# Casting each projection result one tile later in VectorE's order

## The chip, the cores and the metric

The kernel runs on all 8 cores of one Trainium2 chip. Each core computes half of the queries of one of four sequences; the cores don't talk to each other. The metric is the device time in microseconds of the slowest core. Beside the kernel's time a profile of one execution is shown.

## The reference, cut

```python
# x (4, 8192, 1024); Wq, Wk (512, 1024), 8 heads of 64; Wv (8192, 1024)
def attn(x):
    Q = (x @ Wq.T).reshape(b, n, 8, 64)
    K = (x @ Wk.T).reshape(b, n, 8, 64)
    V = (x @ Wv.T).reshape(b, n, 8, 1024)
    a = softmax(einsum('bnhr,bmhr->bhnm', Q, K))
    return einsum('bhnm,bmhd->bnd', a, V)
x = x + layernorm(attn(layernorm(x)))
x = x + layernorm(ffn(layernorm(x)))   # two token-mixed inputs, gate, squared relu
```

## The kernel before

The program is one list of instructions per engine, written out in order; engines meet only at semaphores. `V` is VectorE (DVE), `A` ScalarE (ACT), `T` TensorE (PE), `SY` the SP queue and `G` the POOL queue, both of which only issue DMAs. `V.call(..., chain=True)` also waits for V's own previous instruction. `rec` remembers the semaphore value at which a named step is done, and `waitp(rec[...])` waits for it.

Four phases follow each other, with a meeting of all engines between some of them. Phase 0 transposes the weights. Phase 1, the one that the change touches, handles 97 tiles of 128 tokens: 64 tiles of the whole sequence, for K, and 33 of the core's queries, for Q. Phase 2 is attention, phase 3 the feed-forward part.

For tile idx phase 1 does this:
- SP loads the f32 tile (512 KB) into one of 6 buffers `xf`; the load of tile idx waits for the normalization of tile idx-6 (`lncopy`).
- Layernorm in four steps: `ln_s1` (DVE: two bn_stats, one bn_aggr), `ln_s2` (ACT: Ln and Exp for 1/sigma), `ln_s3` (DVE: a 128x1 product, `nmr`), `ln_s4` (ACT: the bf16 tile, into `x_ln` or `qlnb`).
- `p1_tr` (PE): 8 transposes of 128x128 into PSUM banks 2 and 3. They wait for the tile's `lncopy` and for `p1eg` of tile idx-1, that is, for DVE to have copied the previous transposes out.
- `p1_stage`, first half (DVE): two copies of 512 columns from banks 2 and 3 into `xlt[idx % 4]`, each recorded as `p1eg`.
- `p1_mm` (PE): 32 matmuls of 128 columns into bank 4 + idx % 4. They wait for `p1eg` of the tile and for `p1stage` of tile idx-4.
- `p1_stage`, second half (DVE): waits for the matmuls (`p1mm`), and for tile 8g (K) or each even Q tile also for the writes of the group before, then casts the bank into `ktstage` or `qtstage` (`p1stage`).
- After 8 K tiles, or 2 Q tiles, POOL's queue writes the staging buffer to HBM with 4 DMAs and waits until they have landed (`skw`). There is one `ktstage` and one `qtstage`.

The loop in `emit_scalar_vector` is a software pipeline: turn i has `ln_s1` of tile i, `ln_s2` of i-1, `ln_s3` of i-2, `ln_s4` of i-3 and `p1_stage` of i-4. PE's list is `p1_tr(0)`, and then for each idx `p1_tr(idx + 1)`, `p1_mm(idx)`.

All instructions are recorded with the line of one helper, so the profile's rows are told apart by tile names: `pb` is a PSUM bank, `identb` the identity of the transposes, `wkT_p` and `wqT_p` the projection weights.

Of the kernel before, what the change touches and what calls it, by code (L numbers as in the profile page):

```python
# [332 lines left out]
def ln_s1(V, A, M, rec, key, src, par):  # L333
    st6 = M["stats6"][:, par * 12:par * 12 + 12]
    war = rec[("lnae", key[0], key[1] - 4)] if key[1] >= 4 else None
    half = src.shape[-1] // 2
    V.call("bn_stats", st6[:, 0:6], src[:, 0:half], chain=True, inc=None)
    V.waitp(war)
    V.call("bn_stats", st6[:, 6:12], src[:, half:2 * half], chain=True, inc=None)
    V.call("bn_aggr", M["stats2"][:, par * 2:par * 2 + 2], st6, chain=True,  # L340
           inc=None)
    rec[("lnagg", key[0], key[1])] = V.prev


def ln_s2(V, A, M, rec, key, par):
    A.waitp(rec[("lnagg", key[0], key[1])])
    A.call("activation", M["rstd"][:, par:par + 1],
           M["stats2"][:, par * 2 + 1:par * 2 + 2], AF.Ln,
           bias=M["consts"][:, 0:1], chain=True, inc=None)
    A.call("activation", M["rstd"][:, par:par + 1], M["rstd"][:, par:par + 1],  # L350
           AF.Exp, scale=M["consts"][:, 1:2], chain=True, inc=None)
    rec[("lnae", key[0], key[1])] = A.prev


def ln_s3(V, A, M, rec, key, par):
    V.waitp(rec[("lnae", key[0], key[1])])
    if key[1] >= 4:
        V.waitp(rec[("lncp", key[0], key[1] - 4)])
    V.call("tensor_scalar", M["nmr"][:, par:par + 1],
           M["stats2"][:, par * 2:par * 2 + 1], -1.0, M["rstd"][:, par:par + 1],  # L360
           ALU.mult, ALU.mult, chain=True, inc=None)
    rec[("lnnm", key[0], key[1])] = V.prev


def ln_s4(V, A, M, rec, key, src, dst, par):
    A.waitp(rec[("lnnm", key[0], key[1])])
    A.call("activation", dst, src, AF.Identity, bias=M["nmr"][:, par:par + 1],
           scale=M["rstd"][:, par:par + 1], chain=True, inc=None)
    rec[("lncp", key[0], key[1])] = A.prev


def emit_scalar_vector(A, V, M, rec):
# [28 lines left out]
    NP1 = NK + NTILE  # L401

    def p1_src(i):
        return M["xf"][(i + 4) % 6][:]

    def p1_dst(i):
        return (M["x_ln"][:, i * 1024:(i + 1) * 1024] if i < NK
                else M["qlnb"][i % 4][:])

    def p1_stage(idx):  # L410
        for par in range(2):
            V.waitp(rec[("p1tr", idx, 6 + par)])
            V.call("tensor_copy",
                   M["xlt"][idx % 4][:].rearrange("p (j2 two b) -> p j2 two b",
                                                  two=2, b=128)[:, :, par, :],
                   M["banks"][2 + par][:].bitcast(BF16)[:, 0:512].rearrange(
                       "p (c b) -> p c b", b=128),
                   chain=True, inc=None)
            rec[("p1eg", idx, par)] = V.prev
        V.waitp(rec[("p1mm", idx)])  # L420
        pbk = banks[4 + idx % 4]
        if idx < NK:
            V.wait("skw", 16 * (M["NKW0"] + 4 * (idx // 8)))
            g = idx % 8
            dst3 = M["ktstage"][:].rearrange("p (a f) -> p a f", a=4)[:, :, g * 128:(g + 1) * 128]
        else:
            qi = idx - NK
            V.wait("skw", 16 * (M["NKW0"] + 32 + 4 * (qi // 2)))
            dst3 = M["qtstage"][:].rearrange("p (a f) -> p a f", a=4)[:, :, (qi % 2) * 128:(qi % 2) * 128 + 128]
        src3 = pbk[:].rearrange("p (a f) -> p a f", a=4)  # L430
        V.call("tensor_copy", dst3, src3, chain=True, inc=None)
        rec[("p1stage", idx)] = V.prev

    for i in range(NP1 + 4):
        if i < NP1:
            V.wait(f"lxf{(i + 4) % 6}", 16 * (i // 6 + 1))
            ln_s1(V, A, M, rec, ("p1", i), p1_src(i), i % 4)
        if 0 <= i - 1 < NP1:
            ln_s2(V, A, M, rec, ("p1", i - 1), (i - 1) % 4)
        if 0 <= i - 2 < NP1:  # L440
            ln_s3(V, A, M, rec, ("p1", i - 2), (i - 2) % 4)
        if 0 <= i - 3 < NP1:
            j = i - 3
            if j >= NK and j - 4 >= NK:
                A.waitp(rec[("p1tr", j - 4, 7)])
            ln_s4(V, A, M, rec, ("p1", j), p1_src(j), p1_dst(j), j % 4)
            rec[("lncopy", j)] = rec[("lncp", "p1", j)]
        if 0 <= i - 4 < NP1:
            p1_stage(i - 4)

    A.waitp(A.prev)
    A.call("nop", inc="sph")
# [348 lines left out]
def build():  # L801
# [191 lines left out]
    A0 = Eng("a", counts, "safo")  # L993
    V0 = Eng("v", counts, "svo")
    emit_scalar_vector(A0, V0, M, rec)
    emit_dma(Eng("s", counts, "ld"), Eng("g", counts, "skw"), M, rec)
    totals = dict(counts)
# [5 lines left out]
    Ar = Eng("a", counts2, "safo", record=True)  # L1003
    Vr = Eng("v", counts2, "svo", record=True)
    emit_scalar_vector(Ar, Vr, M, rec)
    Sr = Eng("s", counts2, "ld", record=True)
    Gr = Eng("g", counts2, "skw", record=True)
# [70 lines left out]
```

How the kernel before makes its waits and increments, by code:

```python
def replay(eng, sems, ops):  # L92
    for op in ops:
        if op[0] == "w":
            eng.wait_ge(sems[op[1]], op[2])
        else:
            _, meth, args, kwargs, sem, dinc = op
            ins = getattr(eng, meth)(*args, **kwargs)
            if sem is not None:
                ins.then_inc(sems[sem], dinc)
```

## Time and profile before

| | us |
|---|---|
| runs of the kernel | 12242.71 and 12708.11, median 12475.41 |
| profiled execution | 12247.06 |
| its span on the slowest core (shown) | 12245.5 |
| its spans on the 8 cores | 12231.0 to 12245.5 |
| mean granted TensorE clock, all cores | 0.944 |

The span runs from the first to the last instruction of a core. Busy times are of instructions alone, without waits. Matmuls are pipelined, so that a row's mean duration is longer than the distance between two of them. The granted clock is a share of 2.4 GHz: 1.00 is that level, 0.50 is 1.2 GHz. The rows of a timeline merge neighbouring instructions of a kind, and in brackets stands how long the engine was idle before them and what it waited for.

### The profile page before, as it was taken

How to read it: one execution, taken by the hardware profiler on the slowest of the kernel's cores; microseconds unless marked ns; L12 is line 12 of the kernel's file. 1: busy time of each engine (PE TensorE's matmuls, PEld its weight loads, DVE VectorE, ACT ScalarE, POOL GpSimd, SP SyncE). 2: the span in 40 equal slices, each digit the busy share in tenths (PEclk: the TensorE clock that was granted, in tenths of full speed). 3: DMA queues.
4: the chain of work that ended last, by engine and by line, in shares of the span. 5: the costliest groups of instructions: out<-in, count | busy, mean ns of one | idle time of the engine just before them, and what ended most of it. 6: DMA issues, size and time to landing. Idle time of an engine off the chain costs nothing.

```text
span 12245.5 us, 243677 instructions; the slowest of 8 cores (12231.0 to 12245.5 us)
## 1 busy us (share of the span) xinstructions
PE 10725.1 (88%) x89784; PEld 7880.7 (64%) x89784; DVE 5608.9 (46%) x12826; ACT 3302.1 (27%) x9514; POOL 93.9 (1%) x180
## 2 busy tenths in 40 slices
PE   3555999999999999999999999999999999999354
PEld 2444777777676767676767676767676767677222
DVE  4433444444444444444444444444444444445554
ACT  0222222222222222222222222222222222223322
POOL 0001000000000000000000000000000000000000
PEclk9666999999999999999999999999999999999677
DMA  7221111111111111111111111111111111112311
GB/s 237 88 78 60 45 46 47 46 47 47 47 47 47 46 47 46 48 46 48 46 48 46 46 47 43 50 42 52 40 53 41 53 40 53 39 54 79 100 42 49
DMA packets 695446, 681.03 MB, mean 56 GB/s; under 512 B 592448, under 2 KB 608960, under 8 KB 657664
## 3 DMA queue, kind: packets, MB, share of 16 engines
q1 hardware_dynamic: 678592, 595.56, 16.9%
q0 software_dynamic: 15680, 69.87, 1.4%
q8 instruction: 730, 11.96, 0.4%
q14 instruction: 444, 3.64, 0.1%
HBM read 595.44 MB, written 69.86 MB: 54 GB/s over the span
## 4 chain that ended last, share of the span: by engine, by line
PE 85%; DVE 8%; issue 2%; ACT 2%; DMA 2%; DVEq 0%; SPq 0%; ACTq 0%; POOL 0%; POOLq 0%
PE pb L98 85%; DVE stats L98 2%; DVE outsb L98 2%; DVE xlt L98 1%; DVE wstage L98 1%; DMA wvt_s<-wstage 1%; DMA xmb<-xm_s 1%; DVE xrT L98 0%; DVE xkT L98 0%; DVE d L98 0%; DVEq L95 0%; ACT rstd L98 0%; ACT krelu L98 0%; DVE ktstage L98 0%; ACT rgate L98 0%
## 5 line engine op out<-in xcount | busy, mean ns | idle before, releaser
L98 PE MATMUL pb<-pt,x_ln 128*128 128x256 bf16 (+1 forms) x69632 | 8165.2, 271 | 0.0
L98 PEld LDWEIGHTS pb<-pt,x_ln 128*128 128x128 bf16 x69632 | 6331.0, 98 | 1187.4 <-issue 5.4
L98 ACT ACTIVATE pt<-pb 128x256 bf16<-128x256 f32 (+1 forms) x8704 | 2811.8, 374 | 7202.3 <-PE pb L98 5920.2
L98 DVE TENSOR_TENSOR dacc<-dacc,pt 128x256 f32<-128x256 f32 (+1 forms) x8568 | 3576.6, 417 | 1850.6 <-ACT pt L98 1051.8
L98 DVE CAST yt<-pb 128x256 bf16<-128x256 f32 (+1 forms) x1088 | 453.6, 417 | 2633.6 <-PE pb L98 2633.6
L98 PE MATMUL pb<-qtb,ktb 64*128 64x256 bf16 (+1 forms) x8704 | 1221.6, 277 | 178.3 <-ACT pt L98 156.1
L98 PE MATMUL pb<-wvtb,yt 128*128 128x512 bf16 x4224 | 954.3, 379 | 246.9 <-DVE outsb L98 246.9
L98 PEld LDWEIGHTS pb<-qtb,ktb 64*128 64x128 bf16 x8704 | 418.1, 93 | 1072.7 <-issue 1048.0
L98 PEld LDWEIGHTS pb<-wvtb,yt 128*128 128x128 bf16 x4224 | 404.2, 98 | 744.4 <-issue 306.3
L98 DVE SCALAR_TENSOR_TENSOR outsb<-pb,recip,outsb 128x512 f32<-128x512 f32 x462 | 346.9, 751 | 765.7 <-PE pb L98 741.7
L98 PE MATMUL pb<-wvfT,kactT 128*128 128x512 bf16 x512 | 146.4, 457 | 325.4 <-DVE kactT L98 325.4
L98 PEld LDWEIGHTS pb<-wvfT,kactT 128*128 128x128 bf16 x512 | 56.9, 113 | 411.4 <-issue 373.9
L98 PE MATMUL pb<-identb,x_ln 128*128 128x128 bf16 x512 | 74.7, 301 | 263.8 <-DVE xlt L98 254.8
L98 PE MATMUL pb<-identb,wldb 128*128 128x128 bf16 x768 | 112.1, 301 | 207.3 <-DVE wstage L98 182.4
L98 ACT ACTIVATE rstd<-stats,consts 128x1 f32<-128x1 f32 x195 | 57.3, 294 | 870.8 <-DVE stats L98 833.3
L98 ACT ACT_TABLE_LOAD x33 | 42.3, 1283 | 760.5 <-DVE stats L98 734.3
L98 PEld LDWEIGHTS pb<-identb,x_ln 128*128 128x128 bf16 x512 | 49.4, 132 | 286.3 <-issue 286.3
L98 PEld LDWEIGHTS pb<-identb,wldb 128*128 128x128 bf16 x768 | 74.1, 132 | 245.2 <-issue 245.2
L98 PE MATMUL pb<-xlt,wkT_p 128*128 128x128 bf16 x2048 | 224.1, 306 | 0.0
L98 PEld LDWEIGHTS pb<-xlt,wkT_p 128*128 128x128 bf16 x2048 | 216.6, 147 | 0.0
L98 DVE CAST ktstage<-pb 128x512 bf16<-128x512 f32 x64 | 44.3, 692 | 289.9 <-PE pb L98 289.9
L98 PE MATMUL pb<-identb,ub 128*128 128x128 bf16 x264 | 38.4, 300 | 129.3 <-DVE uTall L98 86.3
(55 smaller groups left out, 2455.4 us busy)
## 6 DMA issues: line engine op xcount, KB each, us to landing
wvtb<-wvt_s SPq DMA_DIRECT2D x272, 1024.0 KB, 9.6
ktb<-kt_s SPq DMA_DIRECT2D x1088, 128.0 KB, 3.2
xmb<-xm_s SPq DMA_DIRECT2D x65, 512.0 KB, 3.7
xf<-xb SPq DMA_DIRECT2D x64, 512.0 KB, 4.1
wldf<-wv SPq DMA_DIRECT2D x64, 512.0 KB, 5.1
xf<-xq SPq DMA_DIRECT2D x33, 512.0 KB, 4.0
xqb<-xq SPq DMA_DIRECT2D x33, 512.0 KB, 6.7
xm_s<-xqb POOLq DMA_DIRECT2D x33, 512.0 KB, 2.9
```

Source lines behind the costliest of these rows:

```text
L98: ins = getattr(eng, meth)(*args, **kwargs)
```

## The change

`p1_stage` is cut in two. Its first half, the two copies out of the transposes' banks, becomes `p1_evac` and stays at tile i-4 of turn i. The second half, with the wait for the matmuls and the cast, keeps its name and moves to tile i-5. In DVE's list of turn i the cast of tile i-5 now follows the copies of tile i-4. The loop gets one more turn. The lists of the other engines stay as they are.

```diff
-    def p1_stage(idx):
+    def p1_evac(idx):
         for par in range(2):
             V.waitp(rec[("p1tr", idx, 6 + par)])
             V.call("tensor_copy",
@@
                    chain=True, inc=None)
             rec[("p1eg", idx, par)] = V.prev
+
+    def p1_stage(idx):
         V.waitp(rec[("p1mm", idx)])
         pbk = banks[4 + idx % 4]
@@
-    for i in range(NP1 + 4):
+    for i in range(NP1 + 5):
@@
         if 0 <= i - 4 < NP1:
-            p1_stage(i - 4)
+            p1_evac(i - 4)
+        if 0 <= i - 5 < NP1:
+            p1_stage(i - 5)
```

## Rows read from the trace of the kernel before

**Rows 1.** The page: PE's busy tenths in 40 slices of the span.

```profile
PE   3555999999999999999999999999999999999354
```

**Rows 2.** Busy time by stage; the last columns are granted clock, DMA share, GB/s.

```profile
0.00:316.00 316.00, 109.82 (x753) 72.57 (x753) 146.12 (x284) 0.00 (x0) 5.65 (x14) 1.00 0.73 231
316.00:876.00 560.00, 289.12 (x2584) 265.54 (x2584) 224.26 (x469) 123.10 (x203) 15.93 (x30) 0.62 0.25 83
876.00:1147.20 271.20, 145.62 (x1312) 134.06 (x1312) 103.02 (x216) 55.49 (x89) 35.64 (x68) 0.60 0.21 69
1147.20:11620.00 10472.80, 9871.95 (x83440) 7236.60 (x83440) 4821.11 (x11229) 2952.95 (x8939) 20.76 (x39) 0.98 0.17 49
```

**Rows 3.** Timeline of one K tile: start us, us, engine, instructions.

```profile
606.42 3.62 PE L98 MATMUL pb<-xlt,wkT_p 128*128 128x128 bf16 x32
...
610.28 0.69 DVE L98 CAST ktstage<-pb 128x512 bf16<-128x512 f32 x1 [4.71 <-PE pb L98]
611.08 1.49 DVE L98 BATCH_NORM_STATS2 stats<-xf 128x6 f32<-128x512 f32 x2
...
613.03 0.29 ACT L98 ACTIVATE rstd<-stats,consts 128x1 f32<-128x1 f32 x1 [6.67 <-DVE stats L98]
613.30 0.95 DVE L98 COPY xlt<-pb 128x512 bf16<-128x512 bf16 x2
...
613.80 1.24 ACT L98 ACTIVATE x_ln<-xf,nmr,rstd 128x1024 bf16<-128x1024 f32 x1
```

**Rows 4.** Waits from 300 to 1200 us: total, times, longest.

```profile
DVE ktstage L98 <- PE pb L98: 289.9, 64, 4.7
...
DVE qtstage L98 <- PE pb L98: 148.9, 33, 4.7
```

**Rows 5.** Timeline: copies of tiles 2 and 92, the last cast; a chain piece.

```profile
339.79 0.95 DVE L98 COPY xlt<-pb 128x512 bf16<-128x512 bf16 x2
...
1116.31 0.95 DVE L98 COPY xlt<-pb 128x512 bf16<-128x512 bf16 x2
...
1146.47 0.69 DVE L98 CAST qtstage<-pb 128x512 bf16<-128x512 f32 x1 [3.60 <-PE pb L98]
...
724.83 4.33 PE pb L98 x39
```

**Rows 6.** Busy time and granted clock in short stretches (columns as in rows 2).

```profile
616.00:617.00 1.00, 1.00 (x12) 1.00 (x11) 0.00 (x0) 0.00 (x0) 0.00 (x0) 0.50 0.75 205
...
618.00:619.00 1.00, 0.34 (x7) 0.17 (x3) 0.48 (x1) 0.00 (x0) 0.00 (x0) 1.00 0.11 45
...
621.00:622.00 1.00, 0.00 (x0) 0.00 (x0) 0.75 (x3) 0.59 (x2) 0.00 (x0) 0.60 0.00 0
...
1140.00:1140.70 0.70, 0.70 (x15) 0.70 (x14) 0.00 (x0) 0.00 (x0) 0.00 (x0) 0.97 0.00 0
```

**Rows 7.** A K group's last cast and its writes; all K writes: ns, landing.

```profile
396.42 0.69 DVE L98 CAST ktstage<-pb 128x512 bf16<-128x512 f32 x1 [4.48 <-PE pb L98]
...
397.64 2.14 POOL L98 DMA_DIRECT2D kt_s<-ktstage  x4 [76.07 <-DVE ktstage L98]
...
L98 POOL DMA_DIRECT2D kt_s<-ktstage x32: 539/539/544, 397.6 to 877.1; - x32
...
DMA to landing us min/median/max: 2.5/3.1/4.4
```

**Rows 8.** The same for Q.

```profile
1010.90 0.69 DVE L98 CAST qtstage<-pb 128x512 bf16<-128x512 f32 x1 [4.40 <-PE pb L98]
...
1012.12 2.13 POOL L98 DMA_DIRECT2D qt_s<-qtstage  x4 [14.94 <-DVE qtstage L98]
...
DMA to landing us min/median/max: 1.7/1.8/2.8
```

**Rows 9.** DMA landing of all input tiles.

```profile
DMA to landing us min/median/max: 3.7/4.0/8.3
```

**Rows 10.** The page: casts out of PSUM in attention.

```profile
L98 DVE CAST yt<-pb 128x256 bf16<-128x256 f32 (+1 forms) x1088 | 453.6, 417 | 2633.6 <-PE pb L98 2633.6
```

## The prediction

> **What bounds the kernel now.** The page's 40 slices come first [rows 1]: TensorE (PE) is busy 9 tenths in most of them, but only 5 in slices 2 to 4. The busy time by stage [rows 2] gives the stages their edges: weights to 316 us, the layernorm and K/Q projection (phase 1, the loop that the change touches) from 316 to 1147.2, attention to 11620. Only phase 1 is touched, so 831 us are at stake and the 11,100 us behind it should stand. In phase 1 PE is busy 435 of 831 us and VectorE (DVE) 327: neither is full.
>
> The timeline of one tile says why [rows 3]. DVE casts the K result out of PSUM (610.28), does the next tile's statistics, the small scale, and copies the next transposes out (613.30); PE, idle since 610.04, starts when the first of these copies is done, runs 8 transposes and 32 matmuls, and DVE idles until the last matmul. The two engines take turns. The waits in this stretch say the same [rows 4]: DVE's cast waited for PE 289.9 us in 64 K tiles and 148.9 us in 33 Q tiles (4.5 us each). A turn is a closed ring: cast, statistics, copy, transposes, matmuls, cast. From the copy of tile 2 to that of tile 92 it takes (1116.31 - 339.79) / 90 = 8.63 us a tile [rows 5].
>
> **The change, part by part.** No instruction, byte or wait is added or removed. In DVE's queue the cast of tile i-1 now stands behind the copies of tile i; before, the cast of tile i stood there. One more turn of the loop drains the pipe.
>
> *The cast's wait.* PE's order is transposes(i+1), matmuls(i). Before, DVE could not reach the statistics until matmuls(i) had ended. Now it waits for matmuls(i-1), which PE starts right behind transposes(i), while DVE copies. The ring still exists, but it now spans two tiles: cast(i-1), statistics, copy(i+1), transposes(i+2), matmuls(i+1), cast(i+1). So three lower bounds for the pitch of a tile:
> - DVE alone: from cast to the end of the copies 613.30 + 0.95 - 610.28 = 3.97 us [rows 3], and the 0.10 us that lies between two dependent DVE instructions in the same rows: 4.07 us.
> - PE alone at the 1.2 GHz level: the rest of a tile behind its first transpose, 39 instructions with the last one's 0.3 us to its end, is one piece of 4.33 us in the chain of work [rows 5]; back to back a tile then takes some 0.107 us an instruction, 4.3 us. At 2.4 GHz, 15 matmuls touch a stretch of 0.70 us, some 3 of them still from before it: 0.055 to 0.06 each [rows 6], 2.3 us for 40.
> - The ring over two tiles: half of 8.63, 4.32 us at the level that the trace has now; with 2.3 us for PE it is (3.97 + 2.3 + 0.4 for the hand-overs) / 2 = 3.3 us.
>
> *Which level.* Now the granted clock is at 0.50 through most of each burst, rises to 1.00 at a burst's end and falls back some 3 us later, while PE has nothing to do [rows 6]; over phase 1 it is 0.61 [rows 2]. After the change PE at 1.2 GHz would be busy without a pause; that is more than what raised it in the rows, so I take the 2.4 GHz level, at which PE's pauses are 4.07 - 2.3 = 1.8 us, shorter than the roughly 3 us of pause before the fall in the rows. I choose 4.07 us: DVE bound. From copy(2), which the change does not move (cast(0) still waits for matmuls(0) and ends at 337.46), to copy(92): 339.79 + 90 x 4.07 = 706.1.
>
> *The staging buffer, late next.* The casts write a single buffer; each 8 K tiles (each 2 Q tiles) POOL's queue sends it out by 4 DMAs, and the next cast waits until they have landed. That is hidden today under 4.5 us of waiting for PE; now the cast comes 4.07 - 0.69 = 3.38 us after the one before it has ended. K: cast ends 397.11, POOL issues from 397.64, the fourth 3 x 0.535 later, lands 3.1 us on: 402.3, 5.2 us behind the cast [rows 7]. Wait 1.8 us, 8 times (the last at the first Q tile): 14.4 us. Q: cast ends 1011.59, POOL from 1012.12, 1.6, and 1.8 to landing: 1015.5, 3.93 us [rows 8]. Wait 0.55 us, 13 times before tile 92: 7.2 us. Everything behind the cast on DVE (the statistics, the next copy, and with it PE) waits along, so these count in full. PE then pauses 1.8 + 1.8 us, more than the pause before the fall in the rows, so I let the clock fall; one tile at the lower level costs 4.3 + 0.3 for the hand-overs against 4.07, some 0.5 us, 8 times, 4 us. Copy(92) starts at 706.1 + 14.4 + 7.2 + 4 = 731.7.
>
> *The tail.* Tiles 93 to 96 have no statistics; two buffer round trips of 3.93 us pace them: cast(92) waits until 5.7 us behind copy(92), copies and casts of 93 to 95 follow and end at 15.0, and cast(96) waits 3.93 more and takes 0.69: 19.6. Phase 1's last cast ends at 751.3 instead of 1147.16 [rows 5]: 395.9 us less.
>
> *What else runs on each queue.* ScalarE needs 2.0 us a tile (613.03 to 615.04 in [rows 3]), half the new pitch; the normalized tile is ready 1 us behind the copy and PE wants it a whole pitch later, so 3 us are left. Input tiles: the SP queue loads tile j+6 when j is normalized; it is read 4 pitches after the statistics that stood in that turn, 16.3 - (615.04 - 611.08) = 12.3 us for a landing of 4.0 us, at most 8.3 [rows 9]. Per tile 512 KB come in and 128 KB go out, 0.655 MB in 4.07 us, 161 GB/s; the weight stage moved 231 GB/s [rows 2]. Hidden. DVE now reads PSUM while PE writes it: in attention, where PE is busy 94% of the time [rows 2], a cast of 256 columns takes 417 ns [rows 10], in phase 1 one of 512 columns with PE idle 0.69 us [rows 3]: 256 columns more for 0.27 us, 1.07 ns each, which leaves 0.14 us fixed for either. No slowing is visible, and I add nothing; if each DVE instruction took 5% longer, it would be 90 x 3.35 x 0.05 = 15 us.
>
> The profiled execution took 12247.06 us (span 12245.5). Forecast: 12247.06 - 395.9 = 11851.2 us, 3.2% less. The median shown, 12475.41, is the mean of 12242.71 and 12708.11; I forecast against the profiled time, which agrees with the first.
>
> **The rivals.**
> - *The clock stays low* (chance 0.14). For it: no row shows 2.4 GHz held in this stage. Then PE and the two-tile ring bound at 4.32 to 4.34 us: 90 x 0.27 = 24 us more, 11875.
> - *POOL is held up by DVE* (0.07). DVE will run without a pause, where now it rests half the time. Against it: POOL's issues lie beside DVE's statistics and copies already and took 539 to 544 ns each [rows 7]. If each of 4 issues had to sit out one 0.69 us DVE instruction, a round trip grows by 2.8 us, and 8 + 16 of them by 66 us: 11917. The Trainium skill, page SBUF — State Buffer, section SBUF: two separate sides, warns of this: descriptors of a GpSimd-issued DMA can't be written while VectorE holds the shared port in a two-port mode. No row of this stage shows such a block.
> - *It is slower than before: the same round trip, much longer* (0.02). It must grow until 24 waits eat the gain: 395.9 / 24 = 16.5 us on top of 5.2 and 3.9. With 8 cores writing and reading at twice the rate a landing of 20 us would do it, say 12,300 us; the longest landings of these writes are 4.4 and 2.8 us [rows 7, 8].
> - *No change* (0.04): another order on PE's or ScalarE's side keeps the engines in turns, 12,247. What speaks against it is that transposes(i+1) wait only for copy(i) and a tile that has been normalized a turn ago. Input tiles that starve DVE belong here too: landings would have to pass 12.3 us.
>
> **How the numbers follow.** Forecast 0.73, the rivals 0.14, 0.07, 0.02, 0.04. The likeliest one's own range: without the staging waits and the clock's share in them 11851 - 26 = 11825, and with a tail without its two round trips (2 x 3.93) 11817; with the landings at their longest (8 x 1.3 + 15 x 1.0 = 25 us) 11876. With the low clock on top, 11900; with POOL held up, 11917. The range is 11815 to 11925. Faster by over 2% (below 12,002, about what a measurement of this kernel can tell) are the first three cases, 0.94, less 0.01 for a partial version of the third; within 2% 0.05; slower 0.02.
>
> **What would show it.** The last Q cast ends near 751 us; a plain tile's pitch is 4.07 us with DVE's rows back to back and its waits for PE gone; new waits of the cast for the K and Q writes, 1.8 us 8 times and 0.55 us 16 times; granted clock above 0.9 in phase 1; attention as long as before. Wrong would be: a pitch of 4.3 us at 0.5 (low clock), POOL instructions over 0.54 us (held up), waits of the statistics for input tiles (starved), or DVE instructions longer than 694, 425 and 692 ns (contention in PSUM, which I priced at nothing).

## The result

The changed kernel's profiled execution took 11889.87 us against 12247.06. Over the timed runs of both kernels the ratio is 0.9708, with a 95% interval of 0.9666 to 0.9749: 2.9% faster, where 3.2% was forecast. The plain median of its 11 runs is 13087.1 us (of the 10 runs of before 13630.17), far outside the stated range of 11,815 to 11,925. In most runs of either kernel the cores of one die or of both had a lower mean granted clock and took longer; the ratio rests on the other runs, which for the changed kernel took 11882.58 to 11889.87 us.

The slices of the page after, to be laid beside [rows 1]: PE, then the granted clock.

```profile
span 11888.3 us, 243701 instructions; the slowest of 8 cores (11875.8 to 11888.3 us)
...
PE   3569999999999999999999999999999999999344
...
PEclk9989999999999999999999999999999999999677
```

Busy time by stage of the changed kernel (columns as in [rows 2]; the stage ends at 794 instead of 1147):

```profile
0.00:316.00 316.00, 111.41 (x763) 73.61 (x764) 147.40 (x286) 0.00 (x0) 5.65 (x14) 1.00 0.74 235
...
316.00:790.00 474.00, 277.69 (x3883) 254.25 (x3882) 325.44 (x680) 178.63 (x292) 50.07 (x95) 0.89 0.41 134
790.00:11260.00 10470.00, 9866.35 (x83306) 7237.06 (x83445) 4819.23 (x11225) 2950.28 (x8935) 22.23 (x42) 0.98 0.16 49
```

DVE's 325 us of work are the same; the stage around them shrank from 831 to 478. PE's busy time fell from 435 to 278 with the same instructions, as the granted clock rose from 0.61 to 0.89. Attention is as long as before.

One K tile in the changed kernel, the counterpart of [rows 3]:

```profile
501.14 0.95 DVE L98 COPY xlt<-pb 128x512 bf16<-128x512 bf16 x2
...
502.19 0.69 DVE L98 CAST ktstage<-pb 128x512 bf16<-128x512 f32 x1
...
502.24 0.55 PE L98 MATMUL pb<-identb,x_ln 128*128 128x128 bf16 x7 [0.31 <-DVE xlt L98]
...
502.62 1.95 PE L98 MATMUL pb<-xlt,wkT_p 128*128 128x128 bf16 x32
...
502.99 1.49 DVE L98 BATCH_NORM_STATS2 stats<-xf 128x6 f32<-128x512 f32 x2
...
505.22 0.95 DVE L98 COPY xlt<-pb 128x512 bf16<-128x512 bf16 x2
```

From copy to copy it is 4.08 us. The cast has no wait in brackets any more; it stands right behind the copies, while PE does the transposes, and PE's 32 matmuls take 1.95 us under DVE's statistics. Durations of DVE's instructions did not change by a nanosecond worth naming (692, 694 and 425 ns).

The waits of the changed kernel from 300 to 800 us, the counterpart of [rows 4]:

```profile
PE pb L98 <- DVE xlt L98: 186.9, 161, 7.8
...
DVE ktstage L98 <- DMA kt_s<-ktstage: 39.8, 7, 6.7
...
DVE qtstage L98 <- DMA qt_s<-qtstage: 27.2, 13, 4.5
...
DVE qtstage L98 <- PE pb L98: 4.9, 3, 2.7
DVE qtstage L98 <- DMA kt_s<-ktstage: 4.8, 1, 4.8
...
DVE ktstage L98 <- PE pb L98: 3.9, 8, 0.6
```

The casts' 439 us of waiting for PE are down to 9. In their place stand 72 us of waiting for the staging buffer's writes: 44.6 for K (39.8 + 4.8) and 27.2 for Q. The forecast had 14.4 for K and 7.2 for Q ahead of the tail. What the landing of these writes has become shows the size of the miss, K first, then Q, beside [rows 7, 8]:

```profile
DMA to landing us min/median/max: 3.5/5.6/7.4
...
DMA to landing us min/median/max: 1.7/2.5/4.2
```

These are core 0, on which the K writes landed latest. On the other seven cores the median for K is 4.2 to 5.4 us (before the change 2.8 to 3.2 on all eight) and the casts waited 35 to 43 us for K.

### The profile page after: what moved, and what is told of

Read it like the earlier page. It is cut to its first block, busy times and chain, and to the rows that moved or that the text cites. A ratio compares the mean times of both kernels' runs of the same rounds, so it can differ in the third digit from the quotient of the medians.

```text
span 11888.3 us, 243701 instructions; the slowest of 8 cores (11875.8 to 11888.3 us)
## 1 busy us (share of the span) xinstructions
PE 10555.5 (89%) x89616; PEld 7736.2 (65%) x89784; DVE 5608.9 (47%) x12826; ACT 3302.5 (28%) x9514; POOL 93.9 (1%) x180
## 4 chain that ended last, share of the span: by engine, by line
PE 84%; DVE 8%; DMA 2%; issue 2%; ACT 2%; DVEq 0%; POOL 0%; SPq 0%; ACTq 0%; POOLq 0%
PE pb L98 84%; DVE stats L98 2%; DVE outsb L98 2%; DVE wstage L98 1%; DMA wvt_s<-wstage 1%; DMA xmb<-xm_s 1%; DVE xrT L98 1%; DVE xkT L98 1%; DVE xlt L98 0%; DVE d L98 0%; DMA kt_s<-ktstage 0%; ACT krelu L98 0%; ACT rstd L98 0%; DVEq L95 0%; DMA qt_s<-qtstage 0%
## 5 line engine op out<-in xcount | busy, mean ns | idle before, releaser
L98 PE MATMUL pb<-wvtb,yt 128*128 128x512 bf16 x4088 | 925.0, 379 | 254.0 <-DVE outsb L98 246.9
L98 DVE BATCH_NORM_STATS2 stats<-xf 128x6 f32<-128x512 f32 x194 | 134.7, 694 | 21.3 <-DVE stats L98 0.9
L98 DVE COPY wstage<-pb 128x512 bf16<-128x512 bf16 x176 | 74.8, 425 | 139.7 <-DMA wvt_s<-wstage 70.9
L98 PE MATMUL pb<-xlt,wkT_p 128*128 128x128 bf16 x2048 | 137.9, 231 | 0.0
```

The lines of the kernel that those rows point to most:

```text
L98: ins = getattr(eng, meth)(*args, **kwargs)
```

## The experiments

Two theories for the dearer waits: the writes now share the DMA engines with the core's own input loads, which come twice as often (A), or VectorE, which no longer rests, holds up POOL's issuing (B). Behind that stood the two larger claims of the forecast, that DVE's own 4.07 us are the bound and that the clock would rise.

### Two staging buffers

```diff
-            V.wait("skw", 16 * (M["NKW0"] + 4 * (idx // 8)))
+            V.wait("skw", 16 * (M["NKW0"] + 4 * max(idx // 8 - 1, 0)))
-            dst3 = M["ktstage"][:]...
+            dst3 = M["ktstage"][(idx // 8) % 2][:]...
```

and the same for `qtstage` and in the DMAs.

> The changed kernel with two K and two Q staging buffers instead of one each; a cast waits for the write of the group before the last. Theory A (the 38 us that the forecast missed are the casts' waits for the staging writes, 44.6 us for K, 27.2 us for Q and 8 more in the tail, and nothing else): all waits of the cast for DMA vanish, copies of tiles 2 and 92 lie 90 x 4.07 = 366 us apart, the end comes 60 to 75 us earlier than in the changed kernel, 11,815 to 11,830 us. Theory B (the DMA engines are the bound, the waits only show where the time goes): input loads become late instead, the statistics wait for them, and the time falls by less than 25 us.

11821.08 us in the profiled execution, 11826.49 in a second one, against 11882.58 to 11889.87 for the changed kernel: 56 to 69 us less. No cast waits for a DMA any more. These are the casts' only waits left:

```profile
DVE qtstage L98 <- PE pb L98: 3.4, 4, 1.6
...
DVE ktstage L98 <- PE pb L98: 1.9, 2, 1.4
```

The copies of tiles 2 and 92 lie 367.9 us apart, against 366.3 for 90 times 4.07:

```profile
341.45 0.95 DVE L98 COPY xlt<-pb 128x512 bf16<-128x512 bf16 x2
...
709.34 0.95 DVE L98 COPY xlt<-pb 128x512 bf16<-128x512 bf16 x2
```

So the waits for the buffer, with the slower clock behind some of them, are the whole of the difference, and the input loads keep up. Theory A of this run holds. K writes still landed in 5.5 us (core 0): two buffers hide the slow landing, they do not mend it.

### Input loads held behind the K writes

```diff
             SY.waitp(rec[("lncopy", idx - 6)])
+        if 16 <= idx <= 72 and idx % 8 == 0:
+            SY.wait("skw", 16 * (M["NKW0"] + 4 * (idx // 8 - 1)))
```

> The changed kernel, single buffers as there; SP issues the input load that comes next behind each K group's last cast (and so those behind it) only when that group's staging write has landed; 8 times, nothing left out. Theory A (the write's landing grew from 3.1 to 5.6 us because the core's own input loads now run beside it on the same 16 DMA engines): landing of the K writes back to about 3.1 us, the cast's wait 8 x 1.8 to 2.2 us instead of 44.6 in all, time 25 to 30 us shorter, near 11,860; the statistics don't wait, since a load has 12 us in hand. Theory B (POOL's issue is held up by VectorE, which no longer rests): landing and waits stay at 5.6 and 5.6 us, time unchanged.

Core 0 of this kernel: POOL's issues and the landing of the K writes.

```profile
L98 POOL DMA_DIRECT2D kt_s<-ktstage x32: 539/539/544, 368.8 to 618.8; - x32
...
DMA to landing us min/median/max: 2.3/3.1/3.7
```

The casts' waits for them:

```profile
DVE ktstage L98 <- DMA kt_s<-ktstage: 17.6, 7, 3.0
...
DVE qtstage L98 <- DMA kt_s<-ktstage: 2.2, 1, 2.2
```

With no load beside it the write lands in 3.1 us, as in the kernel before, and the K waits are 19.8 us instead of 44.6. POOL's issue takes 539 ns in all three kernels. So it is the loads beside the writes (A), not a held-up POOL (B). All eight cores run the same program, so the edit holds back the other cores' loads as well; whether the core's own DMA engines or something that the cores share is the narrow place is not told apart.

The time moved by less than the "25 to 30 us" expected. The four groups of four cores with the changed kernel's mean granted clock (0.965 to 0.966) took 11859.9 to 11877.5 us, a median some 13 us below the changed kernel's 11868.4 to 11892.2. Core 0 gains most: averaged over the eight cores the waits for K fell by 20 us (39.7 to 19.7), those for Q rose by 3, and from the first cast to the last it is 437 us instead of 455. And 19.8 us are more than the 8 x 1.8 of the forecast though the median landing is the same 3.1: a cast waits for the slowest of the four DMAs, not for the median one.

> The changed kernel with the input loads held behind the K writes, as before, to have its time undisturbed. Theory A (the K writes land later because the core's own loads run beside them): casts wait some 20 us for the K writes instead of 44.6, 11,860 to 11,870 us. Theory B (POOL's issue is held up): 11,888.

It gave the same stage again: landing 2.3/2.9/3.6, K waits 13.7 us on core 0, 436 us from the first cast to the last. The expected 11,860 to 11,870 us can be held only against the cores above, the slowest of which took 11871.2 to 11877.5.

What is on the DMA engines meanwhile (columns as in [rows 2]): first the changed kernel, from the issue of a K group's write to the cast that waited for it,

```profile
519.70:527.20 7.50, 3.74 (x62) 3.29 (x59) 2.32 (x7) 1.83 (x3) 2.13 (x4) 1.00 0.93 271
```

then the kernel before, from the issue of such a write to its landing:

```profile
602.80:607.20 4.40, 1.74 (x16) 1.61 (x17) 2.25 (x6) 1.83 (x3) 2.13 (x4) 0.65 0.64 242
```

271 GB/s for 7.5 us are 2.0 MB, of which the group's write is 1.05: two input loads went with it. The engines were busy 0.93 of the time. The loads pay too. The changed kernel's two loads beside the K write of 480.41, then the five that follow behind it:

```profile
L98 SPq DMA_DIRECT2D xf<-xb x2: 328/328/328, 479.6 to 483.7; - x2
...
DMA to landing us min/median/max: 6.5/6.5/6.6
...
L98 SPq DMA_DIRECT2D xf<-xb x5: 328/328/328, 494.3 to 511.1; - x5
...
DMA to landing us min/median/max: 3.2/3.5/4.2
```

Beside the seven K writes from 363 to 597 us the loads of core 0 landed in 4.4 to 6.6 us.

### The writes issued by SP

The 4 DMAs of each group move from POOL's list into SP's, ahead of the next input load, with a semaphore of their own:

```diff
+        if 16 <= idx <= 72 and idx % 8 == 0:
+            kwrite(idx // 8 - 2)
+        if idx >= 74 and idx % 2 == 0:
+            qwrite((idx - 74) // 2)
```

> The changed kernel, single buffers, with the K and Q staging writes issued by the SP queue, each group ahead of the input load that comes next behind its last cast, and not by POOL. Theory A (a write lands late because input loads issued in the same microseconds share the DMA engines with it; who issues it doesn't matter): the load behind it in SP's order starts 1.3 us later and still runs beside the write, so the landing stays above 3.1 us but, with the write first in line, below 5.6; K waits 15 to 40 us instead of 44.6. Theory C (writes issued by POOL are served behind those of the SP queue): issued by SP the writes land in about 3 us and the K waits fall to 15 us or less, the time to 11,850 or less.

11858.36 us, 24 to 32 less than the changed kernel, with single buffers. The slowest core's waits, core 7:

```profile
DVE ktstage L98 <- DMA kt_s<-ktstage: 25.4, 7, 4.8
...
DVE qtstage L98 <- DMA qt_s<-qtstage: 11.6, 6, 3.7
...
DVE qtstage L98 <- DMA kt_s<-ktstage: 3.6, 1, 3.6
```

The landing of the K writes, on core 7 and on core 0:

```profile
DMA to landing us min/median/max: 2.3/4.1/5.4
...
DMA to landing us min/median/max: 2.0/2.8/4.9
```

The cores disagree. On core 7 the waits for K are 29.0 us, in theory A's range, but this core had only 35.1 and a landing of 4.4 us in the changed kernel. On core 0 they fell from 44.6 to 16.4, with a landing of 2.8 instead of 5.6. Over the eight cores they are 14.0 to 29.2 us, two of them under theory C's 15, and the cores took 11831.1 to 11856.8 us, on both sides of its 11,850. The Q writes landed in 1.7 us, as in the kernel before. So A alone, by which it doesn't matter who issues the write, isn't borne out, and C only in part.

A share of the gain is not landing at all: SP's first write comes 0.08 us behind the cast's end and its fourth 1.33 us later (core 0, 398.97), POOL's 0.53 and 1.59 (changed kernel, 402.26). That is 0.7 us a round trip; for 8 K and 13 Q groups I estimate 15 us of casts' waits from it. And with the writes first, the loads behind them pay on core 7: 4.7 to 6.7 us to landing in six groups, where the changed kernel had 3.5 to 5.3. Whether the rest is the order or the queue this run does not tell apart.

### Two buffers in the kernel before

The edit of the first experiment, made in the kernel before.

> The kernel before with the same two buffers each. Both theories: the staging write was hidden there, so nothing moves, 12,247 us within 10. If the time fell, the write's round trip was on the path already.

Cores 4 to 7 took 12230.7 to 12241.1 us, and cores 0 to 3 of a second execution 12232.1 to 12243.2; in the kernel before the cores took 12231.0 to 12245.5. As expected, nothing moved: the round trip was hidden there.

### More matmuls in the kernel before

```diff
         rec[("p1mm", idx)] = T.prev
+        for j in range(28 if idx < NK + NTILE - 4 else 0):
+            T.call("matmul", banks[j % 2][:, 0:128], wT[:, 0:128],
+                   M["identb"][:], start=True, stop=True)
```

> The kernel before with 28 matmuls of 128 columns more behind each tile's projection, into banks that nobody reads; they fill 1.6 to 3.0 us of TensorE's 4 us pause. Theory A (part of the gain is TensorE's clock: with less pause it stays at 2.4 GHz, and a tile's 40 instructions take 2.5 instead of 4.4 us on the path): granted clock in phase 1 from 0.61 to near 1, a turn 6.6 instead of 8.63 us, 12,247 - 97 x 2.0 = 12,050 us. Theory B (the gain is overlap alone): no gain, 12,247 or a little more.

Cores 0 to 3 took 12082.9 to 12096.5 us, 150 less than before, for 28 useless matmuls a tile. Phase 1 on core 0:

```profile
331.00:997.00 666.00, 419.74 (x6476) 393.56 (x6476) 317.21 (x664) 173.35 (x282) 51.05 (x96) 0.95 0.28 92
```

The granted clock is 0.95, the median turn 6.64 us, the mean 6.94 against 8.53. The forecast of 12,050 was 40 us too good: in some turns the clock was at 0.50 again, as in the one from 506.44 to 514.59, which took 8.15 us. So the clock is worth 1.6 us a tile where PE and DVE take turns, and 150 of the 357 us of the change could be had without any overlap.

### The cast ahead of the copies

```diff
-        if 0 <= i - 4 < NP1:
-            p1_evac(i - 4)
         if 0 <= i - 5 < NP1:
             p1_stage(i - 5)
+        if 0 <= i - 4 < NP1:
+            p1_evac(i - 4)
```

> The changed kernel with the two steps of a turn swapped: the cast of tile i-5 stands ahead of the copies of tile i-4, not behind them. Theory A (what counts is that the cast comes a tile late; the order within a turn only decides how much cover TensorE has): the matmuls then have only the statistics as cover, 2.4 us against 2.5 at 2.4 GHz and 4.4 at 1.2, so a turn takes 4.1 to 4.3 us while the clock holds and up to 6.3 while it doesn't; the staging waits now also delay the copies of the same turn: 11,900 to 12,050 us. Theory B (the order within the turn carries the gain): near 12,247.

Cores 0 to 3 took 11997.5 to 12007.4 us, inside A's range. On core 0:

```profile
DVE ktstage L98 <- PE pb L98: 96.3, 56, 2.5
...
DVE qtstage L98 <- PE pb L98: 61.7, 28, 4.4
```

and over the stage:

```profile
331.00:910.00 579.00, 373.75 (x3872) 340.85 (x3872) 317.83 (x665) 173.66 (x282) 51.24 (x96) 0.69 0.33 105
```

The turn's median is 5.95 us. Lateness alone brings 238 of the 357 us; the last third needs the cast behind the copies, where PE has a full turn of cover. With less cover each turn has some pause of both engines, and the clock stays at 0.69 of 2.4 GHz.

### The cast on ScalarE

```diff
-        V.waitp(rec[("p1mm", idx)])
+        A.waitp(rec[("p1mm", idx)])
...
-        V.call("tensor_copy", dst3, src3, chain=True, inc=None)
-        rec[("p1stage", idx)] = V.prev
+        A.call("activation", dst3, src3, AF.Identity, chain=True, inc=None)
+        rec[("p1stage", idx)] = A.prev
```

on top of the two buffers.

> The changed kernel with two staging buffers each, and the cast moved from VectorE's list to the same place of ScalarE's. Theory A (with the casts' waits gone a tile costs what VectorE's own instructions cost, 4.07 us): without the 0.69 us cast and its 0.10 us gap the pitch is 3.28 us, 90 x 0.79 = 71 us less than with two buffers alone (11,821): near 11,750; ScalarE has 2.0 + 0.7 us a tile. Theory B (the input loads or TensorE bound right behind 4.07 us): the pitch stays above 3.6 us, the time above 11,780, and the statistics wait for loads or the copies for TensorE.

11754.1 us. The same kernel once more:

> Two staging buffers and the cast on ScalarE once more, for an undisturbed profile and an interval: 11,754 us again, a pitch of 3.28 us, ratio to the kernel before 0.960.

The profiled execution took 11753.03 us, another one 11751.88. One tile of it:

```profile
500.98 0.95 DVE L98 COPY xlt<-pb 128x512 bf16<-128x512 bf16 x2
501.28 0.60 ACT L98 ACTIVATE ktstage<-pb 128x512 bf16<-128x512 f32 x1 [0.58 <-PE pb L98]
...
504.26 0.95 DVE L98 COPY xlt<-pb 128x512 bf16<-128x512 bf16 x2
```

3.28 us from copy to copy, as worked out; 0.79 us taken off DVE's list came off the tile in full, and 68 of the 71 us off the whole. That is the direct test that DVE's own instructions are the bound. Beside the 12247.06 of the kernel before it makes 0.960, the best version here; it is a ratio of two executions, without an interval.

## Why the prediction was right or wrong

**Right: the mechanism and the pitch.** The ring over two tiles, DVE as the bound at 4.07 us (measured 4.08), no slower DVE instructions beside PE's writes into PSUM, the statistics never waiting for an input tile, attention unchanged. The last experiment shows the bound by moving it.

**Right: the level of the clock.** 0.89 over the stage instead of 0.61. It falls where the forecast let it fall, behind a K group's wait. On the changed kernel, single microseconds through such a wait:

```profile
524.00:525.00 1.00, 0.96 (x18) 0.78 (x15) 0.00 (x0) 0.00 (x0) 0.00 (x0) 1.00 1.02 250
...
527.00:528.00 1.00, 0.00 (x0) 0.00 (x0) 0.76 (x2) 0.00 (x0) 0.00 (x0) 1.00 0.31 123
...
530.00:531.00 1.00, 0.05 (x1) 0.08 (x1) 0.73 (x3) 0.81 (x3) 0.00 (x0) 0.50 0.04 8
```

PE was done at 525, and the level was 0.50 at 530. The price was forecast as 4 us and is 6.4, DVE's waits for PE between the copies of tiles 2 and 92 (casts 5.5, copies 0.9). The rival of a low clock throughout did not come about.

**Wrong in size: the staging buffer, late next.** The step "K: ... lands 3.1 us on" took the median landing, from a trace in which the write ran alone. In the kernel before, one load is issued each 8.5 us, and behind the cast that ends at 601.94 it comes at 606.43, when the write's bytes have nearly all moved; at a pitch of 4.07 us two loads fall into the write (issued at 519.25, just ahead of it, and one turn later). I had worked out the mean rate, 161 GB/s against 231, and wrote "Hidden". That answered whether the loads keep up, which they do, and not what a burst of 1.05 MB behind which the cast stands would wait for. The median was the wrong number besides: the cast waits for the slowest of the four, which landed 3.7 to 4.4 us behind its issue in the kernel before. In the changed kernel it is 5.7 to 7.4 (core 0). The copies of tiles 2 and 92 and the last cast of the changed kernel:

```profile
336.59 0.95 DVE L98 COPY xlt<-pb 128x512 bf16<-128x512 bf16 x2
...
772.64 0.95 DVE L98 COPY xlt<-pb 128x512 bf16<-128x512 bf16 x2
...
793.28 0.69 DVE L98 CAST qtstage<-pb 128x512 bf16<-128x512 f32 x1 [4.46 <-DMA qt_s<-qtstage]
```

The sum from copy 2 to copy 92:

| | forecast | measured |
|---|---|---|
| 90 turns of 4.07 | 366.3 | 366.3 |
| K writes | 14.4 | 44.6 |
| Q writes up to tile 92 (27.2 - 3.9 - 4.5 in the tail) | 7.2 | 18.8 |
| clock, waits for PE | 4.0 | 6.4 |
| sum | 391.9 | 436.1 (336.59 to 772.64: 436.05) |

The tail took 21.3 us instead of 19.6, the stage began 3.2 us earlier on this core, so the last cast ended at 793.97 instead of 751.3. Of these 42.7 us 38.7 arrived in the end (11889.87 - 11851.2); the rest, spread over the later stages, was not looked into. Doubled buffers take the term away whole, which shows what it is; held loads take K's from 44.6 to 19.8 on this core, which shows that the loads beside the write made most of it. How a load slows a write, by sharing the engines or by the order in which they are served, stays open, and so does what made Q's more than double (its writes landed in 2.5 us instead of 1.8).

The rival "POOL is held up by DVE" would have cost 66 us more with another cause. POOL's issues took 539 ns as before with DVE busy all through, and with the loads held the landing was back at 3.1 us; the rule of the Trainium skill (page SBUF — State Buffer, section SBUF: two separate sides) that the prediction told was not seen at work with these DVE instructions.

That 11889.87 lies within the range is luck: the likeliest case alone reached only to 11876, and the range went to 11925 for a low clock and a held-up POOL, which didn't come about.

**Wrong: which time was forecast.** The step "I forecast against the profiled time" settled on the better of two runs that lay 3.8% apart, and the range was made of mechanisms of phase 1 alone. The median of the changed kernel's runs is 13087.1 us, 1162 above the range's end, and a range meant for it needed a term of that size. It says nothing of the change: the kernel before has a median of 13630.17.

**A slip with little effect.** [rows 5] calls 339.79 the copy of tile 2; before the change it is that of tile 1. The pitch before is thus (1116.31 - 339.79) / 91 = 8.53 us, not 8.63. In the changed kernel the copies at this place are those of tile 2, so the sum stands; only the ring over two tiles comes to 4.27 instead of 4.32 us, below the 4.3 us of PE alone.

## What to carry to other kernels

Where two engines take turns, look for the one instruction that waits for the result of its own turn, and let it come a turn later, behind the instruction that the other engine waits for; the order within the turn was worth a third of the gain here. Then ask what ran alone only because the loop was slow: a landing read from a half idle loop is no price for the full one, the wait goes by the slowest DMA of a group and not by the median, and a single staging buffer that was free becomes the next wait. A clock that had been low because the engine paused comes back with the overlap, and belongs in the sum.

## What was not expected of the hardware

- A POOL-issued write of 4 x 256 KB landed in 3.1 us alone and 4.2 to 5.6 us (medians of the cores) beside input loads. The median over all loads hides what it cost them: it is 3.8 us against 4.0 before, but those beside a K write took 4.4 to 6.6 on core 0. Issued by SP ahead of the loads, Q's writes were back at 1.7 us, and K's at 2.7 to 4.1 by core. Why is open.
- 28 matmuls a tile whose result nobody reads made a kernel 150 us faster, by the clock alone.
- The trace of before shows a granted clock of 1.00 up to 348 us, but the 32 matmuls of the first tile (332.9 to 336.2) came 0.107 us apart, the pace of 1.2 GHz; before the first change of level the column does not tell the clock.
